# Attention probabilities in fp16 halves for all four key tiles: four in-place exponentials instead of two, and another order of scores on TensorE

## The chip, the cores and the metric

The kernel runs on one core of a Trainium2 chip. The metric is the device time of one execution in microseconds (us). TensorE (PE) multiplies, VectorE (DVE), ScalarE (ACT) and GpSimd (POOL) work on its results, SyncE (SP) issues the transfers. Matmuls write to PSUM, which has eight banks of 128 x 512 float32; everything else lies in SBUF.

## What is computed

Two transformer layers over x (2 batches x 512 rows x 512), each with modulated layer norms, attention and a feed-forward part. The change lies in the attention of layer 1:

```python
q_c = (c_q @ Wq_up).reshape(b, s, 128, 4);  q_r = (x @ Wq_rope).reshape(b, s, 128, 64)
k_c = (c_kv @ Wk_up).reshape(b, s, 128, 4); v_c = (c_kv @ Wv_up).reshape(b, s, 128, 4)
k_r = x @ Wk_rope
scores = (einsum('bqhd,bkhd->bhqk', q_c, k_c) + einsum('bqhd,bkd->bhqk', q_r, k_r)) / sqrt(68)
attn = softmax(scores);  out = einsum('bhqk,bkhd->bqhd', attn, v_c);  out @ Wo
```

There are 128 heads of 4 columns, with no mask: each query of 512 sees all 512 keys of its batch.

## The kernel before

The attention of layer 1 is cut into 128 units. A unit u is one pair of heads in one batch (u % 2). Per unit the scores are made turned, keys on the partitions: four key tiles of 128 keys times two heads give eight "slots" of 128 keys x 512 queries, in the order of the table `SLOTS` (slots 0 to 3 are key tiles 0 and 1, slots 4 and 5 key tile 2, slots 6 and 7 key tile 3). Work is handed on by hand-written semaphores; the order on each engine is that of the code. Nothing is scheduled by a tool.

**TensorE.** Per unit `before_sums` and then `behind_sums` run. Each slot's score is two matmuls into bank s % 4, with float32 operands in their rounded form: `scores1_rope` (L2593) and `scores1_content` (L2600). Between them stand three other kinds of work. `max_scores` (L2578) makes for unit u + 2 eight more score tiles with queries on the partitions, into banks 4 and 5 in turn, from which the row maxima are taken; number i of them waits until the maximum of number i - 2 is taken (`max_done`). `rope_queries` (L2508 to L2510) makes the queries of unit u + 3 in four pieces of three matmuls. `sum_unit` (L2623, L2628) multiplies the exponentials of unit u - 1 with its values into bank 7. It stands at the end of `before_sums`, that is behind slot 3's scores and number 1 of the maxima, and waits for POOL's semaphore `p_split` and DVE's `p_low`.

**The halves.** In the first 96 units (`HALVED`), the exponentials of key tiles 0 to 2 are split into two fp16 parts, high and rest, and multiplied with values that carry three bfloat16 parts in their columns: 12 matmuls of 128x32 by 128x512 (L2623). Key tile 3 is multiplied in float32, by 4 matmuls of 256 columns (L2628, two records each in the trace). Outputs go to four groups of 32 rows of bank 7.

**ScalarE** takes the exponential of each slot (L1413). Slots 0 to 3, 6 and 7 go to SBUF (x or pT, in turn by unit). Slots 4 and 5 (`IN_PLACE`) go back into their bank, and ScalarE copies them at once to fp16 (L1420). The high parts of slots 2 and 3 are ScalarE's too (L1424), behind slot 3. Ahead of a unit's exponentials it copies the rope queries of unit u + 2 (L1373, L1374, `q_high`).

**VectorE** takes the maxima of the eight tiles of unit u + 2 (L1934, called reduction i below), and makes the rest of slots 4 and 5 of unit u from the bank (L1925, `unit_low`), one behind reduction 4 and one behind reduction 5. Then comes one transposition (L1946) and the rest of the next rope queries (L1886, L1887, `q_low`). In every second unit there is a cast of weights (L1807) behind reduction 1. `unit_low` waits for the exponential of the slot behind its own, since only then has ScalarE's copy been made.

**GpSimd** makes both parts of slots 0 and 1 (L923, L925), prepares the values of the next unit, and makes the rests of slots 2 and 3 (L934), the last work for a unit's `sum_unit`.

Of the kernel before, what the change touches and what calls it, by code (L numbers as in the profile page):

```python
# [9 lines left out]
F16 = mybir.dt.float16  # L10
# [38 lines left out]
HTILES = 3  # L49
IN_PLACE = (4, 5)  # L50
# [21 lines left out]
def adaln_two_layers(nc, a, out):  # L72
# [8 lines left out]
    with ctx:  # L81
# [175 lines left out]
        halved_part = lambda par, s, i: pH[:, par, s, i] if s < 4 else pH_late[:, par, s - 4, i]  # L257
# [462 lines left out]
        def _(pool):  # L720
# [131 lines left out]
            def zero_others():  # L852

                pool.wait_ge(f_added, NT)
                pool.memset(ost[0:1, 0], 1.0).then_inc(zeroed, 1)
                pool.memset(vp[:], 0.0).then_inc(zeroed, 1)
                pool.memset(mcol[:].bitcast(F32), 0.0).then_inc(zeroed, 1)
                pool.wait_ge(zeroed, 3)
                for kp in range(2):
                    ones = slice(OROWS * kp + DEN, OROWS * kp + DEN + HD1)  # L860
                    pool.memset(vp[:, kp, HTILES:TB, :, ones], 1.0).then_inc(zeroed, 1)
                    pool.memset(vpb[:, kp, 0:HTILES, :, ones], 1.0).then_inc(zeroed, 1)

# [33 lines left out]
            def values(v, k, pair):  # L897
# [8 lines left out]
                pool.tensor_copy(vp[:, kp, HTILES:TB, :, OROWS * kp:OROWS * kp + HD1], full[:, HTILES:TB])  # L906
# [10 lines left out]
            def halve(u, k, pair):  # L917

                par = k % 2
                for i in range(2):  # L920
# [3 lines left out]
                    pool.wait_ge(p_split, 4 * u + i + 1)  # L924
# [7 lines left out]
                pool.wait_ge(exp1, 8 * u + 9)  # L932
                for i in range(2, 4):
                    e = pool.tensor_tensor(halved_part(par, i, 1), PT[par][:, i], halved_part(par, i, 0), ALU.subtract)  # L934
                e.then_inc(p_split, 1)
# [6 lines left out]
            pool.wait_ge(zeroed, 7)  # L942
# [148 lines left out]
        def _(act):  # L1091
# [284 lines left out]
            def period(u, k, pair):  # L1376
# [11 lines left out]
                for s in range(8):  # L1388
# [32 lines left out]
                    if s == 3 and exists(u, HALVED):  # L1421
                        act.wait_ge(exp1, 8 * u + 8)
                        for i in (2, 3):
                            act.activation(halved_part(k % 2, i, 0), PT[k % 2][:, i], ACT.Copy)  # L1424
# [86 lines left out]
        def _(dve):  # L1511
# [367 lines left out]
            dve.wait_ge(zeroed, 7)  # L1879
# [47 lines left out]
            def maxima(w, k, use, pair, p, quad):  # L1927


                if exists(w, UNITS):  # L1930
                    wait(dve, m_loaded[k % 2], 32 * use)
                    for i in range(8):
# [5 lines left out]
                        if i in IN_PLACE and exists(w - 2, HALVED):  # L1938
                            unit_low(w - 2, k - 2, i)
# [210 lines left out]
        def _(pe):  # L2150
# [429 lines left out]
            def scores1_rope(u, k, s, use):  # L2580

                if exists(u, UNITS):
# [7 lines left out]
                    if s + 4 in IN_PLACE and exists(u - 1, HALVED):  # L2590
                        pe.wait_ge(p_low, 2 * u - 1 + s)
# [10 lines left out]
            def sum_unit(w, k, pair):  # L2602

                if exists(w, UNITS):
# [12 lines left out]
                    if halved:  # L2617
                        pe.wait_ge(p_split, 4 * w + 4)
                        pe.wait_ge(p_low, 2 * w + 2)
                        for kb in range(HTILES):  # L2620
                            for h in range(2):
                                for half in range(2):
                                    pe.matmul(rows(2 * h + half), vpb[:, k % 2, kb, h], halved_part(k % 2, SLOTS.index((h, kb)), half),  # L2623
                                              start=(kb == 0 and opens), stop=False)
                        for h in range(2):
                            for half in range(2):
                                at = slice(half * S // 2, (half + 1) * S // 2)
                                e = pe.matmul(rows(2 * h + half)[:, at], vp[:, k % 2, HTILES, h], PT[k % 2][:, SLOTS.index((h, HTILES)), at],  # L2628
                                              start=False, stop=closes)
# [29 lines left out]
            def behind_sums(*turn):  # L2659
# [8 lines left out]
                queries(*turn, 1)  # L2668
                maximum(*turn, 4)
                scores(*turn, (6,))  # L2670
                queries(*turn, 2)
                maximum(*turn, 5)
                scores(*turn, (7,))
# [252 lines left out]
```

## Time and profile before

| | |
|---|---|
| three runs | 2174.14, 2176.51, 2177.23 us; median 2176.51 us |
| the profiled execution | 2175.61 us, of which 2173.8 us from the first to the last instruction |
| busy: PE, DVE, ACT, POOL | 98%, 80%, 62%, 62% of the span |
| mean granted clock of TensorE | 0.994 of full speed |

How to read the rows below: each names a line of the kernel, an engine, an operation, what it writes and reads, and how often it stands there in a row (xN). In a timeline the first number is the start, the second the time until the end of the last of the xN. What stands in brackets is the idle time just before, and what ended it. PEld is TensorE's load of weights, which runs beside its matmuls. TensorE's ends are modelled, and its starts are to be trusted more.

### The profile page before, as it was taken

The page shows a single profiled execution, that of the slowest core. Times are in us where ns is not written, and L with a number is a line of the kernel's source. Part 1 is how long each engine was busy: PE and PEld are TensorE (multiplying, and loading weights), DVE is VectorE, ACT ScalarE, POOL GpSimd, SP SyncE. Part 2 cuts the span into 40 slices and gives each one's busy share as a digit, 9 for nine tenths or more (in the row PEclk, how much of TensorE's full clock was granted, in tenths as well). Part 3 has the DMA queues.
Part 4 walks back from the last instruction along what each step waited for, and adds up shares of the span by engine and source line. Part 5 has one row for each costly group of instructions (what it writes and reads, how often), then busy time and mean ns, then how long its engine had stood idle before and what let it go on. Part 6 is the DMA issues. An engine that isn't in the chain of part 4 may idle for free.

```text
span 2173.8 us, 42824 instructions
## 1 busy us (share of the span) xinstructions
PE 2122.4 (98%) x11276; PEld 1644.1 (76%) x11276; DVE 1732.3 (80%) x3095; ACT 1341.9 (62%) x2709; POOL 1357.7 (62%) x1621
## 2 busy tenths in 40 slices
PE   7999999999999999999999999999999999999978
PEld 4788888888886757777777777777777777777756
DVE  6787788788777758888888888888888877788764
ACT  2443443433433568888888888888888865555532
POOL 4766766766753447777777777777777721365334
PEclk9999999999999999999999999999999999999999
DMA  7010010010004153222222222222222222444441
GB/s 249 26 43 30 20 48 29 19 48 29 19 20 121 37 189 108 71 73 78 74 78 65 77 78 74 76 66 79 75 77 69 75 79 76 138 130 124 114 130 40
DMA packets 138991, 165.82 MB, mean 76 GB/s; under 512 B 30261, under 2 KB 72917, under 8 KB 138916
## 3 DMA queue, kind: packets, MB, share of 16 engines
q1 hardware_dynamic: 135076, 152.31, 24.5%
q0 software_dynamic: 3840, 12.59, 2.0%
q8 instruction: 37, 0.61, 0.1%
q14 instruction: 38, 0.31, 0.0%
HBM read 101.52 MB, written 29.10 MB: 60 GB/s over the span
## 4 chain that ended last, share of the span: by engine, by line
PE 87%; DVE 7%; issue 2%; ACT 1%; POOL 1%; SPq 1%; DMA 1%; DVEq 0%; ACTq 0%; POOLq 0%
PE bank L2593 12%; PE bank L2578 11%; PE bank L2600 11%; PE bank L2155 7%; PE bank L2157 7%; PE bank L2156 7%; PE bank L2510 6%; PE bank L2508 5%; PE bank L2509 5%; PE bank L2623 3%; PE bank L2633 3%; PE bank L2628 2%; DVE rope_b L1631 1%; DVE rope_a L1630 1%; DVE rope_b L1632 1%
## 5 line engine op out<-in xcount | busy, mean ns | idle before, releaser
L1934 DVE TENSOR_REDUCE mcol<-bank 128x1 fp32r<-128x512 f32 x1024 | 684.1, 687 | 186.8 <-PE bank L2578 176.7
L2593 PE MATMUL bank<-q,k 128*128 128x512 f32 x1024 | 417.9, 408 | 0.0
L2578 PE MATMUL bank<-km,q 128*128 128x512 f32 x1024 | 406.0, 397 | 3.5 <-ACT q L1374 2.5
L2600 PE MATMUL bank<-q,k 128*128 128x512 f32 x1024 | 404.0, 395 | 0.0
L2578 PEld LDWEIGHTS bank<-km,q 128*128 128x128 f32 x1024 | 317.6, 310 | 53.0 <-DVE mcol L1934 3.9
L1413 ACT ACTIVATE pT<-bank 128x512 f32<-128x512 f32 x416 | 228.1, 602 | 113.7 <-PE bank L2600 111.9
L1413 ACT ACTIVATE x<-bank 128x512 f32<-128x512 f32 x416 | 227.7, 601 | 88.7 <-PE bank L2600 86.5
L2593 PEld LDWEIGHTS bank<-q,k 128*128 128x128 f32 x1024 | 192.3, 188 | 84.7 <-issue 27.9
L2600 PEld LDWEIGHTS bank<-q,k 128*128 128x128 f32 x1024 | 192.9, 188 | 31.7
L2510 PE MATMUL bank<-hT_hi,wr_lo 128*128 128x512 f32 x512 | 205.5, 401 | 0.0
L2508 PE MATMUL bank<-hT_hi,wr_hi 128*128 128x512 f32 x512 | 202.3, 395 | 0.1
L2509 PE MATMUL bank<-hT_lo,wr_hi 128*128 128x512 f32 x512 | 202.1, 395 | 0.0
L850 POOL TENSOR_TENSOR wr_lo<-wst,wr_hi 128x512 fp32r<-128x512 f32 x64 | 82.5, 1289 | 131.1 <-DVE wr_hi L1807 131.1
L2155 PE MATMUL bank<-hT_hi,w_hi 128*128 128x512 f32 x376 | 150.3, 400 | 0.0
L2157 PE MATMUL bank<-hT_hi,w_lo 128*128 128x512 f32 x376 | 148.5, 395 | 0.0
L2156 PE MATMUL bank<-hT_lo,w_hi 128*128 128x512 f32 x376 | 148.4, 395 | 0.0
L744 POOL TENSOR_TENSOR bq_lo<-rope_a,bq_hi 128x512 fp32r<-128x512 f32 x64 | 83.3, 1302 | 82.0 <-ACT bq_hi L1145 82.0
L923 POOL CAST pH<-x 128x512 f16<-128x512 f32 x96 | 58.8, 612 | 118.6 <-ACT x L1413 118.6
L736 POOL TENSOR_TENSOR rope_a<-rope_a,rope_b 128x512 f32<-128x512 f32 x80 | 105.8, 1323 | 43.2 <-DVE rope_b L1632 43.2
L1925 DVE TENSOR_TENSOR pH_late<-bank,pH_late 128x512 f16<-128x512 f32 x192 | 131.3, 684 | 1.5
L1413 ACT ACTIVATE bank<-bank 128x512 f32<-128x512 f32 x192 | 112.0, 583 | 19.7 <-PE bank L2600 19.7
L925 POOL TENSOR_TENSOR pH<-x,pH 128x512 f16<-128x512 f32 x96 | 117.8, 1227 | 7.7
(372 smaller groups left out, 5061.5 us busy)
## 6 DMA issues: line engine op xcount, KB each, us to landing
q<-q SPq DMA_DIRECT2D x256, 128.0 KB, 2.3
wst<-in_L_attn_Wq_rope SPq DMA_DIRECT2D x64, 256.0 KB, 3.1
o_d<-ost SPq DMA_DIRECT2D x63, 256.0 KB, 3.1
st_q<-in_L_attn_wq SPq DMA_DIRECT2D x8, 1024.0 KB, 7.6
st_wo<-in_L_attn_wo SPq DMA_DIRECT2D x8, 1024.0 KB, 5.4
q<-qc_d SPq DMA_DIRECT2D x256, 32.0 KB
km<-kc_d SPq DMA_DIRECT2D x256, 32.0 KB
k<-kc_d SPq DMA_DIRECT2D x256, 32.0 KB
```

What stands on the lines that cost most here:

```text
L1413: act.activation(bank[s % 4][:] if in_place else PT[k % 2][:, s], bank[s % 4][:], ACT.Exp, scale=float((HD1 + ROPE) ** -0.5)).then_inc(exp ...
L1925: dve.tensor_tensor(halved_part(k % 2, s, 1), bank[s % 4][:], halved_part(k % 2, s, 0), ALU.subtract).then_inc(p_low, 1)
L1934: dve.tensor_reduce(mcol[:, k % 2, i % 4, i // 4:i // 4 + 1], bank[4 + i % 2][:], AX.X, ALU.max, negate=True)\
L2155: pe.matmul(ps, lh_, rh, start=(i == 0), stop=False)
L2156: pe.matmul(ps, lh_, rl, start=False, stop=False)
L2157: e = pe.matmul(ps, ll, rh, start=False, stop=(i == n - 1))
L2508: pe.matmul(bank[6][:], wr_hi[:, par, kk], hT_hi[:, kk, at], start=(kk == 0), stop=False)
L2509: pe.matmul(bank[6][:], wr_hi[:, par, kk], hT_lo[:, kk, at], start=False, stop=False)
L2510: e = pe.matmul(bank[6][:], wr_lo[:, par, kk], hT_hi[:, kk, at], start=False, stop=(kk == KT - 1))
L2578: pe.matmul(bank[4 + i % 2][:], q2[:, k % 4, h, i % 4:S:4], km[:, b, h], start=True, stop=True).then_inc(max_mm, 1)
L2593: pe.matmul(bank[s % 4][:], k1[:, k % 2, t], q1[:, k % 4, h], start=True, stop=False)
L2600: pe.matmul(bank[s % 4][:], k2[:, k % 2, h, t], q2[:, k % 4, h], start=False, stop=True).then_inc(scores1, 1)
```

## The change

`HTILES` becomes 4: key tile 3 is multiplied in fp16 halves too, so the 4 float32 matmuls of 256 columns become 4 fp16 ones of 512 columns. `IN_PLACE` becomes slots 2 to 5. Their exponentials stay in their banks; ScalarE makes the high part and VectorE the rest, so VectorE has four of these a unit instead of two. They stand where the new table `LOW_BEHIND` puts them: behind reductions 0, 2, 4 and 5. Slots 6 and 7 go to SBUF as before and are split there: ScalarE casts slot 6 between the exponentials of slots 6 and 7, GpSimd casts slot 7 and makes both rests, once slot 7's exponential is there. The score of slot 6 now waits for the rest of slot 2 (`p_low`), which shares its bank, and that of slot 7 for the rest of slot 3. On TensorE the scores of slots 6 and 7 move ahead of the maxima tiles 4 and 5.

```diff
-HTILES = 3
-IN_PLACE = (4, 5)
+HTILES = 4
+IN_PLACE = (2, 3, 4, 5)
+LOW_BEHIND = {0: 2, 2: 3, 4: 4, 5: 5}
...
-        halved_part = lambda par, s, i: pH[:, par, s, i] if s < 4 else pH_late[:, par, s - 4, i]
+        halved_part = lambda par, s, i: (
+            pH[:, par, s, i] if s < 4 else pH_late[:, par, s - 4, i] if s < 6
+            else PT[par][:, s - 2].bitcast(F16)[:, i * S:(i + 1) * S])
...
-                pool.tensor_copy(vp[:, kp, HTILES:TB, :, OROWS * kp:OROWS * kp + HD1], full[:, HTILES:TB])
...
-                pool.wait_ge(exp1, 8 * u + 9)
-                for i in range(2, 4):
-                    e = pool.tensor_tensor(halved_part(par, i, 1), PT[par][:, i], halved_part(par, i, 0), ALU.subtract)
-                e.then_inc(p_split, 1)
+                pool.wait_ge(exp1, 8 * u + 12)
+                pool.sem_inc(spare, 1)
+                pool.tensor_copy(halved_part(par, 7, 0), PT[par][:, 7]).then_inc(p_split, 1)
+                pool.tensor_tensor(halved_part(par, 6, 1), PT[par][:, 6], halved_part(par, 6, 0), ALU.subtract)
+                pool.wait_ge(p_split, 5 * u + 4)
+                pool.tensor_tensor(halved_part(par, 7, 1), PT[par][:, 7], halved_part(par, 7, 0), ALU.subtract).then_inc(p_split, 1)
...
-                    if s == 3 and exists(u, HALVED):
-                        act.wait_ge(exp1, 8 * u + 8)
-                        for i in (2, 3):
-                            act.activation(halved_part(k % 2, i, 0), PT[k % 2][:, i], ACT.Copy)
+                    if s == 6 and exists(u, HALVED):
+                        act.wait_ge(exp1, 8 * u + 11)
+                        act.activation(halved_part(k % 2, 6, 0), PT[k % 2][:, 6], ACT.Copy)
...
-                        if i in IN_PLACE and exists(w - 2, HALVED):
-                            unit_low(w - 2, k - 2, i)
+                        if i in LOW_BEHIND and exists(w - 2, HALVED):
+                            unit_low(w - 2, k - 2, LOW_BEHIND[i])
...
-                        pe.wait_ge(p_low, 2 * u - 1 + s)
+                        pe.wait_ge(p_low, 4 * u - 1 + s)
+                    if s - 4 in IN_PLACE and exists(u, HALVED):
+                        pe.wait_ge(p_low, 4 * u - 5 + s)
...
-                        for h in range(2):
-                            for half in range(2):
-                                at = slice(half * S // 2, (half + 1) * S // 2)
-                                e = pe.matmul(rows(2 * h + half)[:, at], vp[:, k % 2, HTILES, h], PT[k % 2][:, SLOTS.index((h, HTILES)), at],
-                                              start=False, stop=closes)
...
-                maximum(*turn, 4)
                 scores(*turn, (6,))
+                maximum(*turn, 4)
                 queries(*turn, 2)
-                maximum(*turn, 5)
                 scores(*turn, (7,))
+                maximum(*turn, 5)
                 maximum(*turn, 6)
```

VectorE, one unit with its cast of weights, behind the loop. In the names `mcol` holds the maxima, `pH` and `pH_late` the fp16 parts, `q` the queries. Before:

```order
L1886 TENSOR_TENSOR q<-bank,q 64x512
L1887 TENSOR_TENSOR q<-bank,q 64x512
L1934 TENSOR_REDUCE mcol<-bank 128x1 x2
L1807 CAST wr_hi<-wst 128x512
L1934 TENSOR_REDUCE mcol<-bank 128x1 x3
L1925 TENSOR_TENSOR pH_late<-bank,pH_late 128x512
L1934 TENSOR_REDUCE mcol<-bank 128x1
L1925 TENSOR_TENSOR pH_late<-bank,pH_late 128x512
L1934 TENSOR_REDUCE mcol<-bank 128x1 x2
L1946 STREAM_TRANSPOSE mrow<-mcol 128x4x32
```

The same unit on VectorE, now:

```order
L1889 TENSOR_TENSOR q<-bank,q 64x512
L1936 TENSOR_REDUCE mcol<-bank 128x1
L1927 TENSOR_TENSOR pH<-bank,pH 128x512
L1936 TENSOR_REDUCE mcol<-bank 128x1
L1809 CAST wr_hi<-wst 128x512
L1936 TENSOR_REDUCE mcol<-bank 128x1
L1927 TENSOR_TENSOR pH<-bank,pH 128x512
L1936 TENSOR_REDUCE mcol<-bank 128x1 x2
L1927 TENSOR_TENSOR pH_late<-bank,pH_late 128x512
L1936 TENSOR_REDUCE mcol<-bank 128x1
L1927 TENSOR_TENSOR pH_late<-bank,pH_late 128x512
L1936 TENSOR_REDUCE mcol<-bank 128x1 x2
```

A rest (slot 2's) now stands between reductions 0 and 1, and another (slot 3's) behind reduction 2.

TensorE, the second half of a unit, from maximum tile 3 (L2578) to the last piece of the queries. Before:

```order
L2578 MATMUL bank<-km,q 128x512
L2593 MATMUL bank<-q,k 128x512
L2600 MATMUL bank<-q,k 128x512
L2508 MATMUL bank<-hT_hi,wr_hi 128x512
L2509 MATMUL bank<-hT_lo,wr_hi 128x512
L2510 MATMUL bank<-hT_hi,wr_lo 128x512
L2578 MATMUL bank<-km,q 128x512
L2593 MATMUL bank<-q,k 128x512
L2600 MATMUL bank<-q,k 128x512
L2508 MATMUL bank<-hT_hi,wr_hi 128x512
L2509 MATMUL bank<-hT_lo,wr_hi 128x512
L2510 MATMUL bank<-hT_hi,wr_lo 128x512
```

The same place on TensorE now, from maximum tile 3 (L2580) on:

```order
L2580 MATMUL bank<-km,q 128x512
L2597 MATMUL bank<-q,k 128x512
L2604 MATMUL bank<-q,k 128x512
L2510 MATMUL bank<-hT_hi,wr_hi 128x512
L2511 MATMUL bank<-hT_lo,wr_hi 128x512
L2512 MATMUL bank<-hT_hi,wr_lo 128x512
L2597 MATMUL bank<-q,k 128x512
L2604 MATMUL bank<-q,k 128x512
L2580 MATMUL bank<-km,q 128x512
L2510 MATMUL bank<-hT_hi,wr_hi 128x512
L2511 MATMUL bank<-hT_lo,wr_hi 128x512
L2512 MATMUL bank<-hT_hi,wr_lo 128x512
```

Maximum tile 4 stood six matmuls behind tile 3 and now stands eight behind it, after the scores of slot 6.

GpSimd, the end of one unit's work. Before and now, with the two preparations of values (`l_pad`, `vp`) ahead of it:

```order
L912 CAST vp<-l_pad 128x6x4
L915 TENSOR_TENSOR vp<-l_pad,vp 128x6x4
L934 TENSOR_TENSOR pH<-x,pH 128x512 x2
```

```order
L913 CAST vp<-l_pad 128x8x4
L916 TENSOR_TENSOR vp<-l_pad,vp 128x8x4
L935 CAST x<-x 128x512
L936 TENSOR_TENSOR x<-x 128x512
L938 TENSOR_TENSOR x<-x 128x512
```

The cast of slot 7 has come in ahead of the two rests, and all three now start behind the exponential of slot 7 instead of that of slot 4.

## Rows read from the trace of the kernel before

**Rows 1.** The page, part 1: busy time, share of the span, instructions by engine.

```profile
PE 2122.4 (98%) x11276; PEld 1644.1 (76%) x11276; DVE 1732.3 (80%) x3095; ACT 1341.9 (62%) x2709; POOL 1357.7 (62%) x1621
```

**Rows 2.** Timeline of TensorE around the first and the last halved sum.

```profile
828.25 0.62 PE L2623 MATMUL bank<-pH,vp 128*32 128x512 f16 x8
...
1756.85 0.62 PE L2623 MATMUL bank<-pH,vp 128*32 128x512 f16 x8
```

**Rows 3.** Timeline of TensorE, one sum in the middle of the loop.

```profile
1111.38 0.40 PE L2578 MATMUL bank<-km,q 128*128 128x512 f32 x1
1111.70 0.62 PE L2623 MATMUL bank<-pH,vp 128*32 128x512 f16 x8
1112.15 0.39 PE L2623 MATMUL bank<-pH_late,vp 128*32 128x512 f16 x4
1112.36 0.60 PE L2628 MATMUL bank<-pT,vp 128*32 128x256 f32 x8
1112.90 0.50 PE L2593 MATMUL bank<-q,k 128*128 128x512 f32 x1
1113.24 0.40 PE L2600 MATMUL bank<-q,k 128*128 128x512 f32 x1
```

**Rows 4.** Timeline of VectorE, from reduction 4 to reductions 0 and 1 of the next.

```profile
1106.45 0.69 DVE L1934 TENSOR_REDUCE mcol<-bank 128x1 fp32r<-128x512 f32 x1 [0.70 <-PE bank L2578]
1107.17 0.69 DVE L1925 TENSOR_TENSOR pH_late<-bank,pH_late 128x512 f16<-128x512 f32 x1
1107.84 0.69 DVE L1934 TENSOR_REDUCE mcol<-bank 128x1 fp32r<-128x512 f32 x1
1108.45 0.68 DVE L1925 TENSOR_TENSOR pH_late<-bank,pH_late 128x512 f16<-128x512 f32 x1
1109.05 1.28 DVE L1934 TENSOR_REDUCE mcol<-bank 128x1 fp32r<-128x512 f32 x2
1110.36 0.40 DVE L1946 STREAM_TRANSPOSE mrow<-mcol 128x128 f32<-128x128 f32 x1
1110.86 0.68 DVE L1886 TENSOR_TENSOR q<-bank,q 64x512 fp32r<-64x512 f32 x1
1111.55 0.69 DVE L1887 TENSOR_TENSOR q<-bank,q 64x512 fp32r<-64x512 f32 x1
1112.28 1.29 DVE L1934 TENSOR_REDUCE mcol<-bank 128x1 fp32r<-128x512 f32 x2
```

**Rows 5.** Timeline ahead of the loop, where a maximum tile waits for a reduction.

```profile
790.29 1.28 DVE L1934 TENSOR_REDUCE mcol<-bank 128x1 fp32r<-128x512 f32 x2
...
791.03 0.31 PEld L2578 LDWEIGHTS bank<-km,q 128*128 128x128 f32 x1 [0.94 <-DVE mcol L1934]
...
791.48 0.39 PE L2508 MATMUL bank<-hT_hi,wr_hi 128*128 128x512 f32 x1
```

**Rows 6.** Timeline of ScalarE, from the rope queries to slot 5.

```profile
1109.25 0.59 ACT L1373 ACTIVATE q<-bank 64x512 fp32r<-64x512 f32 x1 [0.34 <-PE bank L2510]
...
1110.47 2.07 ACT L1413 ACTIVATE x<-bank 128x512 f32<-128x512 f32 x4
...
1113.63 0.58 ACT L1408 ACTIVATE ost<-bank 128x512 f32<-128x512 f32 x1
1114.11 0.59 ACT L1413 ACTIVATE bank<-bank 128x512 f32<-128x512 f32 x1
1114.73 0.60 ACT L1420 ACTIVATE pH_late<-bank 128x512 f16<-128x512 f32 x1
1115.29 0.58 ACT L1413 ACTIVATE bank<-bank 128x512 f32<-128x512 f32 x1
```

**Rows 7.** Timeline of GpSimd in the same unit.

```profile
1111.24 0.61 POOL L923 CAST pH<-x 128x512 f16<-128x512 f32 x1 [2.50 <-ACT x L1413]
1111.93 1.16 POOL L925 TENSOR_TENSOR pH<-x,pH 128x512 f16<-128x512 f32 x1
...
1117.62 2.30 POOL L934 TENSOR_TENSOR pH<-x,pH 128x512 f16<-128x512 f32 x2
```

More of the change, by code:

```diff
@@ L860, in zero_others @@
                     ones = slice(OROWS * kp + DEN, OROWS * kp + DEN + HD1)
-                    pool.memset(vp[:, kp, HTILES:TB, :, ones], 1.0).then_inc(zeroed, 1)
                     pool.memset(vpb[:, kp, 0:HTILES, :, ones], 1.0).then_inc(zeroed, 1)
@@ L923, in halve @@
                     pool.tensor_copy(halved_part(par, i, 0), PT[par][:, i]).then_inc(p_split, 1)
-                    pool.wait_ge(p_split, 4 * u + i + 1)
+                    pool.wait_ge(p_split, 5 * u + i + 1)
                     e = pool.tensor_tensor(halved_part(par, i, 1), PT[par][:, i], halved_part(par, i, 0), ALU.subtract)
@@ L941, in _ @@
             pool.wait_ge(vc_ready, NT)
-            pool.wait_ge(zeroed, 7)
+            pool.wait_ge(zeroed, 5)
             values(0, 0, 0)
@@ L1878, in _ @@
             key_low(1)
-            dve.wait_ge(zeroed, 7)
+            dve.wait_ge(zeroed, 5)
             dve.wait_ge(vc_ready, NT)
@@ L2617, in sum_unit @@
                     if halved:
-                        pe.wait_ge(p_split, 4 * w + 4)
-                        pe.wait_ge(p_low, 2 * w + 2)
+                        pe.wait_ge(p_split, 5 * w + 5)
+                        pe.wait_ge(p_low, 4 * w + 4)
                         for kb in range(HTILES):
@@ L2622, in sum_unit @@
                                 for half in range(2):
-                                    pe.matmul(rows(2 * h + half), vpb[:, k % 2, kb, h], halved_part(k % 2, SLOTS.index((h, kb)), half),
-                                              start=(kb == 0 and opens), stop=False)
-                        for h in range(2):
-                            for half in range(2):
-                                at = slice(half * S // 2, (half + 1) * S // 2)
-                                e = pe.matmul(rows(2 * h + half)[:, at], vp[:, k % 2, HTILES, h], PT[k % 2][:, SLOTS.index((h, HTILES)), at],
-                                              start=False, stop=closes)
+                                    e = pe.matmul(rows(2 * h + half), vpb[:, k % 2, kb, h], halved_part(k % 2, SLOTS.index((h, kb)), half),
+                                                  start=(kb == 0 and opens), stop=(kb == HTILES - 1 and closes))
                     else:
@@ L2668, in behind_sums @@
                 queries(*turn, 1)
+                scores(*turn, (6,))
                 maximum(*turn, 4)
-                scores(*turn, (6,))
                 queries(*turn, 2)
+                scores(*turn, (7,))
                 maximum(*turn, 5)
-                scores(*turn, (7,))
                 maximum(*turn, 6)
```

## The prediction, made before the changed kernel had run

> **What bounds the kernel now.** I read the page first: PE is busy 98% of the span, DVE 80%, ACT and POOL 62% [rows 1]. That is a mean over the whole program, so I looked for the stage that the change touches. The first halved sum starts at 828.25 us and the 96th at 1756.85 [rows 2]: 95 units in 928.6 us, 9.775 us each. In the timeline of TensorE inside it, matmul follows matmul. From maximum tile 1 (1111.38) over the sum to the second matmul of slot 4 (1113.24) it is 1.86 us [rows 3]. The other 34 of the 36 full matmuls of a unit then have 9.775 - 1.86 = 7.915 us, 0.2328 us each, with no wait among them. So TensorE alone sets the pace, and what others do is hidden. How well hidden shows on VectorE: it waits 0.70 us for maximum tile 4 [rows 4], but reductions 0 and 1 start at 1112.28, 0.58 us behind the start of the sum, although their tiles were made before it (the second's matmul started at 1111.38 [rows 3]). So VectorE is already late there, and catches up by waiting at tiles 2 to 4. That is where the change puts work.
>
> **TensorE's own work.** The 12 fp16 matmuls run from 1111.70 to 1112.36: three rounds of four column groups, 0.22 us each. The 4 float32 matmuls take from 1112.36 to about 1112.79, and the next full matmul starts at 1112.90, 0.54 behind 1112.36 [rows 3]. The float32 part alone has no row of its own end. I take the way out of the column groups (0.11) as unchanged, so 0.43 goes and one fp16 round of 0.22 comes: 0.21 less. TensorE's floor is 9.565 us. With nothing else changed that would be 95 x 0.21 = 20 us of gain.
>
> **VectorE's work.** Two more rests a unit. A rest is 0.68 to 0.69 us long, but the next operation starts before its end: 1108.45 to 1109.05 is 0.60, and the pair of reductions (1.28 for two of 0.69) gives 0.60 too. Behind reduction 4 I see 0.72 [rows 4]. I take 0.60 to 0.61, since most follow at that, and keep 0.72 for the range. The other steps: from the pair at 1109.05 to the transposition 1.31, so 0.71 from reduction 7; then 0.50, 0.69 and 0.73 to the first reduction [rows 4]. Twelve operations, a transposition and two query rests are 12 x 0.605 + 0.11 + 0.50 + 0.69 + 0.73 = 9.3 us, under 9.565: VectorE has room on average. The question is where its work stands.
>
> **The order, laid out with these rows.** Put 0 at the start of a sum. The second matmul of slot 4 starts at 1.33 (1.54 before, less 0.21). Maximum tile 3 is five matmuls on, 2.49. Tile 4 is now eight behind it, 4.36; tile 5 six behind that, 5.75; tile 7 at 6.92; the next sum at 9.565. A reduction starts 0.43 behind its matmul's start (0.39 and a handoff of 0.04). So reduction 4 starts at 4.79, slot 4's rest at 5.40, reduction 5 with its tile at 6.18, slot 5's rest at 6.79, reductions 6 and 7 at 7.39 and 7.99, transposition 8.70, query rests 9.20 and 9.89, reduction 0 at 10.62. That is 1.05 behind the next sum; it was 0.58. Then slot 2's rest at 1.65 and reduction 1 only at 2.25. Tile 3 shares its bank with tile 1, so it waits for reduction 1's end at 2.94 plus 0.05. TensorE would be there at 2.49: **it waits 0.50 us**. A wait costs more than itself. Where a maximum tile waited for a reduction, its weights were loaded only then (791.03), and the next matmul started 0.45 behind, instead of 0.23 [rows 5]: 0.22 more. Behind tile 3 stand the scores of slots 5 to 7, the other tiles and the queries, all later by 0.72. Since tile 4 is eight behind tile 3, VectorE doesn't catch up: its reduction 4 waits for this tile, and the loop closes. Checked round: reduction 1 0.69 + handoff 0.05 + 0.45 + 7 x 0.2328 + 0.43 = 3.25 to reduction 4; from there to the next reduction 1 7.03 (the list above). The sum is 10.28 a unit. The cast of every second unit falls where VectorE waits for tile 4 (from reduction 1 it is ready at 2.41, with the cast at 2.9, needed at 3.25), so I cost it at nothing; without that cover it is 0.46.
>
> A page of the Trainium skill speaks of the reload: TensorE: Matmul & The Clock Gate, section LDWEIGHTS, has a load depend on the number of columns alone, some 107 ns for 128. By it the loop would be an estimated 10.17 us. The trace disagrees: the maximum tile's load is 0.31 us.
>
> **ScalarE.** It gets one cast more, but the order matters: slot 2's rest waits for the exponential of slot 3, and ahead of that stand now two exponentials and a copy in place of two exponentials. The last query matmul (6.69, end 7.09) releases the two query copies (0.61 each [rows 6]), exponential 0 starts at -1.22 against the next sum, each next 0.49 on (2.07 for four), in place to copy 0.62, copy to the next 0.56 [rows 6]: exponential 3 ends at 1.52. The handoff is 0.05 to 0.18 (GpSimd started 0.18 behind an exponential's end [rows 6, 7]). So slot 2's rest could start at 1.57 to 1.70, and VectorE comes at 1.65: a second loop almost as long, 10.20 to 10.32 when closed through tile 3. I take VectorE's 10.28. The output copy of every second unit (0.48 [rows 6]) stands behind slot 3 and delays slots 4 and 5 only, which have room; nothing. The cast of slot 6 lies in the wait for slot 7's score; nothing as well.
>
> **GpSimd.** It loses the 0.2 us copy of values, and its last work is now a cast and two rests behind exponential 7. Cast to rest 0.69, rest to rest 1.13, the last 1.17 [rows 7], with 0.18 of handoff 3.17 us. Exponential 7 ends at 6.56 (slot 7's second matmul 5.52, +0.44, +0.60), so the sum could start at 9.73 instead of 9.565. In the stalled order both move by 0.72, so the sum is late by 0.17; that fits in the 0.50 in which TensorE would wait at tile 3, and costs nothing. Without that stall it is 0.17 to 0.29 a unit (in units with the output copy exponential 7 ends 0.12 later).
>
> **The sum.** (10.28 - 9.775) x 95 = 48 us slower. Against the profiled execution, 2175.6 + 48 = 2223.6; the median of the runs shown is 0.9 us above it. I say 2224 us. The float32 and fp16 parts are in it already, since the loop no longer passes TensorE's floor. Outside the 96 units nothing moves that I can price: two small memsets go.
>
> **The rivals.**
> 1. VectorE keeps up, and GpSimd sets the sum (the other side). If VectorE's chain from reduction 4 to reduction 1 were 6.53 us or less instead of 7.03, tile 3 would not wait. The point from which the result is no slower is a loop of 9.775. For it: no row shows the new order, and handoffs may be shorter. Against: it needs eleven steps of measured length to be 0.045 shorter each. The unit is then 9.73 to 9.85 by GpSimd's chain, so 2171 to 2183, and I call it no change. Chance 0.07.
> 2. All waits hidden, TensorE at its floor: 9.565, 2155.6 us. For it: the busiest engine does have less work. Against: both VectorE and GpSimd must be faster than their rows. Chance 0.08, with all that is faster.
> 3. Only part of the stall: the reload costs 0.11 as behind the sum, or is absorbed. Then 10.0 to 10.15, 2197 to 2211. This lies in the forecast's own range.
> 4. VectorE doesn't overlap its operations in the new order. Then each next one starts at the former's end. Five pitches on the loop grow from 0.60 to 0.69 (the two ahead of reduction 5 are covered by its wait), 10.28 + 0.45 = 10.73, 2266 us. For it: one rest did follow at 0.72. Against: five rows at 0.60 or near. Chance 0.08, with all that is above 2245.
>
> Rival 4 is what the Trainium skill states in VectorE: DVE Perf Modes, section The DRAIN you can't avoid: the next operation doesn't start until the pipe is empty. The rows of pairs in 1.28 us disagree.
>
> **How the numbers follow.** The forecast, with the stall at tile 3, has 0.77; its own range is 2197 (reload and one handoff less) to 2245 (two pitches of 0.72 a unit, 0.23 more: +22). With 0.77 there and the edges of the others, 2190 to 2245 holds some 0.8. A change of 0.2%, 4 us, is about what a measurement of this kernel can tell from none. Faster 0.08, within 0.2% 0.06, slower 0.86.
>
> **What would show it.** In the new trace the unit should be 10.2 to 10.3 us from sum to sum. TensorE's weight load of the maxima (L2580) should wait for `mcol`, once a unit at tile 3, 0.3 to 0.6 us, and perhaps at tile 2. Reduction 0 should start about 1 us behind the sum, slot 2's rest right behind it. The four matmuls of the new round should be 0.2 us apart from the ones before. GpSimd's last rest should end just about where the sum starts. The prediction is wrong if VectorE's rests are much shorter, if `mcol` isn't waited for, or if the wait stands at the sum itself (GpSimd) or at slots 6 and 7 (the rests of slots 2 and 3, which I have ready over 1 us early).

## The result, and the profile after

The changed kernel takes **2242.88 us** (median of 4 runs, 2240.74 to 2244.87); the kernel before took 2175.32 us. The ratio is 1.031, with a 95% interval of 1.030 to 1.032: 67.6 us slower.

The page after, part 1, as [rows 1]: PE still shows 98%, so the share says nothing of the loss. VectorE's busy time has grown by 120 us.

```profile
PE 2190.2 (98%) x10892; PEld 1631.5 (73%) x10892; DVE 1852.6 (83%) x3287; ACT 1405.1 (63%) x2805; POOL 1399.1 (62%) x1619
```

The timeline of TensorE around the first and the last halved sum, as [rows 2]:

```profile
828.83 0.62 PE L2627 MATMUL bank<-pH,vp 128*32 128x512 f16 x8
...
1815.04 0.62 PE L2627 MATMUL bank<-pH,vp 128*32 128x512 f16 x8
```

Between them lie 95 units in 986.21 us, 10.381 each instead of 9.775. That is 57.6 us of the span's growth of 69.3 (2243.1 against 2173.8). The other 11.7 lie outside: 0.6 before the first sum, 0.7 in the unit in which the halved part ends, 5.8 from the 97th to the 127th sum (312.3 against 306.5 us, 10.41 a unit against 10.22), and 4.6 from there to the end. The stretch from the 97th sum on has no halves at all; only the order of TensorE is new there. (Its means take in two shorter units at the end; a unit in its middle takes 10.65, where it was 10.45.) Most of the last 4.6 us is one wait for a transfer of weights, behind the last sum (TensorE, before and after):

```profile
2080.58 1.97 PE L2732 MATMUL bank<-ident,bw 128*128 128x128 f32 x16 [0.82 <-DMA bw<-in_L_ffn_base_W]
2148.49 2.71 PE L2731 MATMUL bank<-ident,bw 128*128 128x128 f32 x16 [3.98 <-DMA bw<-in_L_ffn_base_W]
```

The mean granted clock behind the 127th sum is also a little lower, 0.91 of full speed against 0.95; both are means of the levels 2.4 and 1.2 GHz. In the runs below this stretch takes between 99.2 and 104.2 us whatever was changed (105.3 here, 100.7 before), so I don't count it to the change.

The places of TensorE's waits in one unit after, as [rows 3] (timelines of PE and PEld, put together in order of time):

```profile
1105.77 0.31 PEld L2580 LDWEIGHTS bank<-km,q 128*128 128x128 f32 x1 [0.29 <-DVE mcol L1936]
1106.23 0.43 PE L2597 MATMUL bank<-q,k 128*128 128x512 f32 x1
...
1108.68 0.62 PE L2627 MATMUL bank<-pH,vp 128*32 128x512 f16 x8
1109.12 0.39 PE L2627 MATMUL bank<-pH_late,vp 128*32 128x512 f16 x4
1109.34 0.39 PE L2627 MATMUL bank<-pT,vp 128*32 128x512 f16 x4
1109.66 0.50 PE L2597 MATMUL bank<-q,k 128*128 128x512 f32 x1
...
1110.23 0.55 PE L2580 MATMUL bank<-km,q 128*128 128x512 f32 x1
1110.61 0.39 PE L2510 MATMUL bank<-hT_hi,wr_hi 128*128 128x512 f32 x1
...
1111.08 0.40 PE L2512 MATMUL bank<-hT_hi,wr_lo 128*128 128x512 f32 x1
1111.47 0.31 PEld L2580 LDWEIGHTS bank<-km,q 128*128 128x128 f32 x1 [0.44 <-DVE mcol L1936]
1111.93 0.39 PE L2597 MATMUL bank<-q,k 128*128 128x512 f32 x1
```

The sum is shorter as laid out: 0.98 from its start to the next full matmul, where it was 1.20. Three places lose more than that. Each is counted as the distance from one start to the next beyond the usual 0.2328. Tile 3 (1111.47): 0.16 of wait and 0.23 of late load. Tile 2 (1110.23): 0.15. Tile 7 (1105.77): 0.23, and 0.04 at the matmul behind. That is 0.81, and 9.565 + 0.81 = 10.375; measured are 10.35 from tile 3 to tile 3 here and 10.381 on the mean.

VectorE in the same stretch (its timeline), from reduction 4 to the cast, as [rows 4]:

```profile
1103.63 0.69 DVE L1936 TENSOR_REDUCE mcol<-bank 128x1 fp32r<-128x512 f32 x1 [0.77 <-PE bank L2580]
1104.23 0.68 DVE L1927 TENSOR_TENSOR pH_late<-bank,pH_late 128x512 f16<-128x512 f32 x1
1105.02 0.69 DVE L1936 TENSOR_REDUCE mcol<-bank 128x1 fp32r<-128x512 f32 x1
1105.63 0.68 DVE L1927 TENSOR_TENSOR pH_late<-bank,pH_late 128x512 f16<-128x512 f32 x1
1106.23 1.28 DVE L1936 TENSOR_REDUCE mcol<-bank 128x1 fp32r<-128x512 f32 x2
1107.54 0.42 DVE L1948 STREAM_TRANSPOSE mrow<-mcol 128x128 f32<-128x128 f32 x1
1107.99 0.68 DVE L1888 TENSOR_TENSOR q<-bank,q 64x512 fp32r<-64x512 f32 x1
1108.68 0.69 DVE L1889 TENSOR_TENSOR q<-bank,q 64x512 fp32r<-64x512 f32 x1
1109.41 0.69 DVE L1936 TENSOR_REDUCE mcol<-bank 128x1 fp32r<-128x512 f32 x1
1110.13 0.69 DVE L1927 TENSOR_TENSOR pH<-bank,pH 128x512 f16<-128x512 f32 x1
1110.74 0.68 DVE L1936 TENSOR_REDUCE mcol<-bank 128x1 fp32r<-128x512 f32 x1
1111.34 0.96 DVE L1809 CAST wr_hi<-wst 128x512 fp32r<-128x512 f32 x1
```

Reduction 1 ends at 1111.42, and tile 3's weights load at 1111.47. Slot 2's rest (1110.13) follows reduction 0 by 0.72, slots 4's and 5's follow theirs by 0.60 and 0.61. The units around it are alike at this place: tile 3's loads stand at 1101.12, 1111.47, 1121.82 and 1132.23. From sum to sum it is less even, 10.2 to 10.6 us in turns of four units, but where one sum is late, the wait at tile 2 behind it is shorter. The pace is set at tile 3, by VectorE.

GpSimd's last three operations before the sum, as [rows 7] (its timeline):

```profile
1105.55 0.61 POOL L935 CAST pT<-pT 128x512 f16<-128x512 f32 x1 [2.48 <-ACT pT L1416]
1106.12 1.17 POOL L936 TENSOR_TENSOR pT<-pT 128x512 f16<-128x512 f32 x1
1107.25 1.18 POOL L938 TENSOR_TENSOR pT<-pT 128x512 f16<-128x512 f32 x1
```

They end at 1108.43, 0.25 ahead of the sum at 1108.68, which is where TensorE comes anyway (0.33 behind tile 1's matmul at 1108.35, as before: 0.32 [rows 3]). So GpSimd is close to being waited for, and isn't in this unit.

Reduction 0 starts 0.73 behind the sum (1109.41), not 1.05 as forecast, because tile 7 has already held the sum back.

### The profile page after: what moved, and what is told of

It reads as the page before. It is cut to its first block, busy times and chain, and to the rows that moved or that the text cites. A ratio compares the mean times of both kernels' runs of the same rounds, so it can differ in the third digit from the quotient of the medians.

```text
span 2243.1 us, 43218 instructions
## 1 busy us (share of the span) xinstructions
PE 2190.2 (98%) x10892; PEld 1631.5 (73%) x10892; DVE 1852.6 (83%) x3287; ACT 1405.1 (63%) x2805; POOL 1399.1 (62%) x1619
## 4 chain that ended last, share of the span: by engine, by line
PE 87%; DVE 7%; issue 2%; ACT 1%; DMA 1%; POOL 1%; SPq 0%; DVEq 0%; ACTq 0%; POOLq 0%
PE bank L2580 14%; PE bank L2597 12%; PE bank L2604 10%; PE bank L2157 7%; PE bank L2159 7%; PE bank L2158 6%; PE bank L2512 5%; PE bank L2511 5%; PE bank L2510 5%; PE bank L2627 4%; PE bank L2632 2%; DVE rope_b L1633 1%; DVE rope_a L1632 1%; DVE rope_b L1634 1%; PE bank L2293 1%
## 5 line engine op out<-in xcount | busy, mean ns | idle before, releaser
L2580 PE MATMUL bank<-km,q 128*128 128x512 f32 x1024 | 450.9, 461 | 4.7 <-ACT q L1377 2.4
L2597 PE MATMUL bank<-q,k 128*128 128x512 f32 x1024 | 419.2, 409 | 0.0
L2580 PEld LDWEIGHTS bank<-km,q 128*128 128x128 f32 x1024 | 307.4, 309 | 129.5 <-DVE mcol L1936 99.7
L2597 PEld LDWEIGHTS bank<-q,k 128*128 128x128 f32 x1024 | 194.5, 190 | 105.5 <-issue 71.8
L1416 ACT ACTIVATE bank<-bank 128x512 f32<-128x512 f32 x384 | 228.2, 594 | 68.7 <-PE bank L2604 67.5
L1416 ACT ACTIVATE pT<-bank 128x512 f32<-128x512 f32 x320 | 180.6, 599 | 72.5 <-PE bank L2604 64.1
L1416 ACT ACTIVATE x<-bank 128x512 f32<-128x512 f32 x320 | 181.0, 599 | 45.9 <-PE bank L2604 37.2
L1927 DVE TENSOR_TENSOR pH<-bank,pH 128x512 f16<-128x512 f32 x192 | 131.4, 684 | 4.8 <-ACT bank L1416 1.9
L1423 ACT ACTIVATE pH_late<-bank 128x512 f16<-128x512 f32 x192 | 114.7, 597 | 6.1
```

Source lines behind the costliest of these rows:

```text
L1416: act.activation(bank[s % 4][:] if in_place else PT[k % 2][:, s], bank[s % 4][:], ACT.Exp, scale=float((HD1 + ROPE) ** -0.5)).then_inc(exp ...
L1927: dve.tensor_tensor(halved_part(k % 2, s, 1), bank[s % 4][:], halved_part(k % 2, s, 0), ALU.subtract).then_inc(p_low, 1)
L2580: pe.matmul(bank[4 + i % 2][:], q2[:, k % 4, h, i % 4:S:4], km[:, b, h], start=True, stop=True).then_inc(max_mm, 1)
L2597: pe.matmul(bank[s % 4][:], k1[:, k % 2, t], q1[:, k % 4, h], start=True, stop=False)
```

## The experiments

All times are medians, with the ratio to the kernel before run on the same chip and its 95% interval. A unit's time is the mean between the first and the 96th halved sum of the profiled execution; "behind" is that from the 97th to the 127th. The ratios of e1 to e4 are to one set of runs of the kernel before, those of e5, e7 and e8 to another, those of e9 and e10 to a third. What stands below about units rests on one profiled execution each.

| run | us | ratio | a halved unit | behind |
|---|---|---|---|---|
| before | 2175.3 to 2177.2 | 1 | 9.775 | 10.22 |
| changed | 2242.9 | 1.031 (1.030 to 1.032) | 10.381 | 10.41 |
| e1_old_order | 2246.0 | 1.032 (1.030 to 1.033) | 10.469 | 10.22 |
| e2_rests_later | 2206.0 | 1.014 (1.012 to 1.017) | 9.994 | 10.41 |
| e3_query_swap | 2233.3 | 1.026 (1.025 to 1.028) | 10.267 | 10.41 |
| e4_before_new_order | 2211.0 | 1.016 (1.015 to 1.018) | 10.061 | 10.41 |
| e5_all_three | 2197.7 | 1.010 (1.008 to 1.012) | 9.994 | 10.17 |
| e7_tile7_later | 2237.1 | 1.028 (1.026 to 1.030) | 10.389 | 10.17 |
| e8_before_tile7_later | 2197.5 | 1.010 (1.007 to 1.012) | 9.985 | 10.17 |
| e9_other_layout | 2174.3 | 0.998 (0.997 to 0.999) | 9.727 | 10.21 |
| e10_slot7_later | 2191.2 | 1.006 (1.004 to 1.008) | 9.928 | 10.20 |

**e1_old_order: the changed kernel with TensorE's old order.**

```diff
-                scores(*turn, (6,))
                 maximum(*turn, 4)
+                scores(*turn, (6,))
                 queries(*turn, 2)
-                scores(*turn, (7,))
                 maximum(*turn, 5)
+                scores(*turn, (7,))
```

> The changed kernel (2242.9 us; 10.38 us a halved unit, 10.26 from sum to sum behind unit 96) with TensorE's old order of the scores of slots 6 and 7 and maximum tiles 4 and 5, everything else as changed. Theory A: the new order puts tile 7 five matmuls (1.16 us) behind tile 5, just as long as the reduction of tile 5 needs (0.43 + 0.69 + 0.05), so its weights are loaded late, 0.2 us a unit in every unit; and it puts tile 4 two matmuls later, on the loop that goes through VectorE. With the old order the units behind 96 should go back to about 10.07, and the halved ones to 10.1 to 10.25 (VectorE's work in units with the cast, or GpSimd's in front of the sum, is next): 2215 to 2225 us. Theory B: the two rests more on VectorE cost all of it and the order nothing: about 2243 us. Theory C: the order was needed so that exponential 7 comes early: the sum waits for GpSimd 0.2 to 0.5 us more, 2245 to 2260 us.

Half of A came: the units behind 96 are back at 10.22, that of the kernel before (not at 10.07). But the halved ones got slower, 10.47, and the whole, 2246.0, is no faster than the changed kernel; that is theory C's time. The waits of the weight loads over one unit and a little more:

```profile
1108.59 0.31 PEld L2580 LDWEIGHTS bank<-km,q 128*128 128x128 f32 x1 [0.46 <-DVE mcol L1936]
1116.19 0.12 PEld L2627 LDWEIGHTS bank<-pH,vp 128*32 128x32 bf16 x8 [0.51 <-POOL pT L938]
1118.84 0.31 PEld L2580 LDWEIGHTS bank<-km,q 128*128 128x128 f32 x1 [0.45 <-DVE mcol L1936]
```

Tile 7 is no longer there. Tile 3 still waits, and now the sum waits for GpSimd (0.51 idle, where 0.25 is usual), as theory C says. That wait isn't what sets the unit, since tile 3 behind it still waits for VectorE. VectorE itself waits for ScalarE (their timelines, put together):

```profile
1106.51 0.59 ACT L1416 ACTIVATE bank<-bank 128x512 f32<-128x512 f32 x1
1107.25 0.69 DVE L1927 TENSOR_TENSOR pH<-bank,pH 128x512 f16<-128x512 f32 x1 [0.21 <-ACT bank L1416]
...
1116.77 0.59 ACT L1416 ACTIVATE bank<-bank 128x512 f32<-128x512 f32 x1
1117.50 0.69 DVE L1927 TENSOR_TENSOR pH<-bank,pH 128x512 f16<-128x512 f32 x1 [0.40 <-ACT bank L1416]
1118.11 0.68 DVE L1936 TENSOR_REDUCE mcol<-bank 128x1 fp32r<-128x512 f32 x1
1118.71 1.30 DVE L1809 CAST wr_hi<-wst 128x512 fp32r<-128x512 f32 x1
```

In every halved unit slot 2's rest starts 0.14 to 0.15 behind the end of slot 3's exponential. This is the prediction's second loop, and it closes: 0.61 to reduction 1, 0.68 + 0.05 to tile 3, 4.41 to the last query matmul, 0.44 to ScalarE's copy of the queries, 3.33 to exponential 3, 0.59 + 0.14 to the next rest, together 10.25. The units without a cast take just that, 10.24 to 10.28. Those with a cast take about 10.67: the cast (1118.71) lasts 1.30, reduction 2 behind it is late, and tile 4's load waits as well, 0.42 in all. In the changed kernel tile 4 comes two matmuls later and its load doesn't wait. So in the halved units the new order more than pays for itself, by 0.09 a unit, though not through GpSimd.

**e2_rests_later: slot 2's and 3's rests behind reductions 2 and 3.**

```diff
-LOW_BEHIND = {0: 2, 2: 3, 4: 4, 5: 5}
+LOW_BEHIND = {2: 2, 3: 3, 4: 4, 5: 5}
```

> The changed kernel with the rests of slots 2 and 3 behind reductions 2 and 3 instead of 0 and 2. Theory A (the stall at maximum tile 3 is what slot 2's rest between reductions 0 and 1 costs): TensorE no longer waits 0.4 us at tile 3 and loads its weights in time; what is left is tile 7's late load, GpSimd in front of the sum and perhaps slot 6's score waiting for slot 2's rest: 9.85 to 10.05 us a halved unit, 2190 to 2210 us. Theory B (VectorE has simply too much work, wherever it stands): the wait moves to slot 6's or slot 7's score at the same size, 10.3 to 10.4 a unit, 2235 to 2245 us.

Theory A: 0.39 us a unit comes back, 37 us in all, with the same number of operations on VectorE. The wait at tile 3 is gone; its load starts one matmul ahead again:

```profile
1112.28 0.31 PEld L2580 LDWEIGHTS bank<-km,q 128*128 128x128 f32 x1
```

Both rests were moved, but tile 3 waits for reduction 1, and only slot 2's rest stood in front of that. So it was the place of this rest, between reductions 0 and 1, that cost 0.39 of the 0.61.

**e3_query_swap: the query rest on the upper partitions first.**

```diff
-                    dve.tensor_tensor(q1[ROPE:P, k % 4, 0], bank[6][0:ROPE], q2[0:ROPE, k % 4, 0].bitcast(F32), ALU.subtract)
                     dve.tensor_tensor(q1[0:ROPE, k % 4, 1], bank[6][ROPE:P], q2[ROPE:P, k % 4, 1].bitcast(F32), ALU.subtract)\
+                    dve.tensor_tensor(q1[ROPE:P, k % 4, 0], bank[6][0:ROPE], q2[0:ROPE, k % 4, 0].bitcast(F32), ALU.subtract)\
                        .then_inc(q1_split, 1)
```

> The changed kernel with the two rests of the rope queries on VectorE in the other order, so that the last one before reduction 0 reads the lower partitions. Slot 2's rest follows reduction 0 at 0.72 us in the changed kernel, others at 0.60. Theory A: it is held until reduction 0 has ended because the last operation that read SBUF (the query rest on the upper 64 partitions) started in another group of partitions. Then the swap gives 0.60, 0.12 us less on the loop: 10.25 a halved unit, about 2231 us. Theory B: the 0.72 is a wait for ScalarE's exponential of slot 3: it stays, and the time too, 2243 us.

Theory A: 10.381 to 10.267, 0.114 less, where 0.12 was forecast. The timelines of VectorE and ScalarE:

```profile
1109.46 0.59 ACT L1416 ACTIVATE bank<-bank 128x512 f32<-128x512 f32 x1
1109.59 0.69 DVE L1936 TENSOR_REDUCE mcol<-bank 128x1 fp32r<-128x512 f32 x1
1110.20 0.69 DVE L1927 TENSOR_TENSOR pH<-bank,pH 128x512 f16<-128x512 f32 x1
```

The rest now follows by 0.61. The 0.72 was not a wait for ScalarE but VectorE holding an operation until the one before it had ended. The Trainium skill has this rule, in VectorE: DVE Perf Modes, section "Two Vector instructions with no wait between them": an operation is held, among other cases, if its first SBUF input starts in another group of 32 partitions than that of the last operation that read SBUF. Reduction 0 reads PSUM alone, so the query rest on the upper 64 partitions was still the last one. The trace agrees, with this swap. It also agrees with the 0.72 behind reduction 4 in [rows 4]: that unit has no cast, which reads SBUF from partition 0 on. In the kernel before, slot 4's rest follows reduction 4 by 0.61 in all 47 halved units with a cast and by 0.72 in 47 of 48 without one.

The swap gave all that it could. Exponential 3 ends at 1110.05 and the rest starts 0.15 behind it, where 0.14 is what e1 shows of a rest that waits for it: the loop through ScalarE now closes at the same length as VectorE's.

**e4_before_new_order: the kernel before with the new order alone** (the diff of e1 the other way round).

> The kernel before with only TensorE's new order of scores and maximum tiles. Theory A: tile 7 waits for the reduction of tile 5 and its weights load late, 0.2 to 0.25 us in each unit, since TensorE is the bound there: halved units 9.98 to 10.02, the units behind about 10.26, together 22 + 6 us: 2200 to 2206 us. Theory B: the order costs nothing by itself: 2175 us.

Theory A in kind, with more in size: 35 us, 0.286 a halved unit, where 0.21 to 0.25 was forecast. Put into the kernel before, the order alone costs more than half of what the whole change does. Timeline of that kernel:

```profile
1105.48 0.63 PE L2578 MATMUL bank<-km,q 128*128 128x512 f32 x2
...
1105.91 0.69 DVE L1934 TENSOR_REDUCE mcol<-bank 128x1 fp32r<-128x512 f32 x1
...
1106.66 0.31 PEld L2578 LDWEIGHTS bank<-km,q 128*128 128x128 f32 x1 [0.29 <-DVE mcol L1934]
```

Tile 5's matmul starts at 1105.48, its reduction at 1105.91 and ends at 1106.60; tile 7's load at 1106.66. TensorE would have come to tile 7's matmul at 1106.64 (1105.48 + 5 x 0.2328), so there is no wait to speak of. But the weights of a matmul that isn't held load one matmul earlier, beside the one before (its load then starts 0.23 ahead). Here they start with the wait's end, and the next matmul comes 0.22 to 0.29 late.

**e7_tile7_later: the changed kernel, tile 7 behind the next unit's slot 0.**

```diff
-                scores(*turn, range(3))
+                scores(*turn, (0,))
+                max_scores(turn[0] + 1, turn[1] + 1, 7, turn[2](1))
+                scores(*turn, (1, 2))
...
-                maximum(*turn, 7)
```

> The changed kernel with maximum tile 7 alone moved behind the next unit's score of slot 0. Theory A: in the halved units TensorE's late load at tile 7 lies beside VectorE's longer chain, which sets the pace through tile 3; so its removal gives nothing there (10.33 to 10.40 a unit), and 0.19 us in each of the units behind 96: 2233 to 2239 us. Theory B: the late loads add up, 0.26 us a unit comes back: 10.12, 2210 to 2218 us.

Theory A, in both stretches: 10.389 instead of 10.381, and 10.17 instead of 10.41 behind. A stall of 0.27 us on the busiest engine was taken away in every halved unit, and nothing came back there. It lay beside VectorE's chain, and TensorE only waited longer at tile 2 (mostly 0.38 to 0.45 in the waits of its loads, where it was at most 0.28).

**e8_before_tile7_later: the same in the kernel before with the new order.**

> The kernel before with the new order of scores and maximum tiles, and tile 7 moved behind the next unit's score of slot 0. With the new order alone it took 2211 us, 10.06 a halved unit. Theory A: all of that is tile 7, which is five matmuls behind tile 5; seven behind, its weights load in time, and the unit is 9.775 again: 2173 to 2178 us. Theory B: another part of the order (tile 4 later, slots 6 and 7 earlier) costs some of it: 2185 us or more.

Theory B. Of the 0.286 only 0.076 comes back. The timeline shows what is next:

```profile
1105.94 0.69 DVE L1934 TENSOR_REDUCE mcol<-bank 128x1 fp32r<-128x512 f32 x1
1106.55 0.68 DVE L1925 TENSOR_TENSOR pH_late<-bank,pH_late 128x512 f16<-128x512 f32 x1
1107.15 1.28 DVE L1934 TENSOR_REDUCE mcol<-bank 128x1 fp32r<-128x512 f32 x2
...
1110.32 1.29 DVE L1934 TENSOR_REDUCE mcol<-bank 128x1 fp32r<-128x512 f32 x2
...
1111.07 0.31 PEld L2578 LDWEIGHTS bank<-km,q 128*128 128x128 f32 x1 [0.18 <-DVE mcol L1934]
```

Reduction 5 starts 1105.94. Behind it seven operations go without a gap to reduction 0, which ends at 1111.01, and tile 2 waits for that. Tile 2 to tile 5 on TensorE and tile 5 to its reduction close the loop. Its length is 4.38 (reduction 5 to reduction 0) + 0.69 + 0.15 to tile 2's matmul (1111.16) + 4.32 to tile 5's (1115.48) + 0.43 = 9.97, the unit. The new order puts two more matmuls between tiles 2 and 5, and this loop becomes longer than TensorE's own work, even with the two rests a unit of the kernel before.

**e5_all_three: e2, e3 and e7 together.**

> The changed kernel with three mends at once: the rests of slots 2 and 3 behind reductions 2 and 3, the query rests in the other order, and maximum tile 7 moved behind the next unit's score of slot 0 (seven matmuls behind tile 5 instead of five). Theory A: what is left of the stalls of the run with later rests (9.99 us a unit) is tile 7's late load (0.26) and GpSimd in front of the sum (up to 0.17); without the first the unit is 9.70 to 9.80, the units behind 96 are back at about 10.22: 2167 to 2180 us, no better than before though TensorE has 0.2 us less to do. Theory B: VectorE's work itself (9.7 to 9.8 us a unit with the cast) or GpSimd's is the bound beyond that: 9.85 to 9.95, 2182 to 2195 us. Theory C: with the stalls gone TensorE's floor of 9.565 shows: 2156 us.

None of the three in full; B's mechanism was nearest, but in which order VectorE's chain closes was still open. The unit is 9.994, exactly that of e2, although the hold and tile 7's late load are gone. It is the loop of e8 again: tile 2 waits 0.39 to 0.44 for reduction 0.

**e9_other_layout: tile 5, and slots 6 and 7, earlier.** On top of e5 (shown is TensorE's order behind the sum; the table puts the rests of slots 2 and 3 both behind reduction 2):

```diff
-                scores(*turn, (4,))
+                scores(*turn, (4, 5))
                 maximum(*turn, 2)
                 queries(*turn, 0)
                 maximum(*turn, 3)
-                scores(*turn, (5,))
                 queries(*turn, 1)
-                scores(*turn, (6,))
                 maximum(*turn, 4)
-                queries(*turn, 2)
-                scores(*turn, (7,))
+                scores(*turn, (6, 7))
                 maximum(*turn, 5)
+                queries(*turn, 2)
                 maximum(*turn, 6)
                 queries(*turn, 3)
```

> The changed kernel with tile 7 behind the next unit's slot 0 and the query rests swapped, as in the run with three mends, but laid out so that tiles 4 to 7 and slots 6 and 7 all come early: TensorE does slots 4 and 5 together, tiles 2 and 3, two query pieces, tile 4, slots 6 and 7 together, tile 5; VectorE makes the rests of slots 2 and 3 one behind the other after reduction 2. Theory A: the run with three mends was held at 9.99 us a unit by the chain from tile 5's reduction through seven more VectorE operations to reduction 0 and tile 2, because the new order puts tile 5 late; here tile 5 is 3 matmuls earlier and tile 2 two later, GpSimd gets exponential 7 0.7 us earlier, and the unit comes to VectorE's total of 9.6 to 9.75: 2160 to 2176 us. Theory B: VectorE's total with its cast beside GpSimd is the bound at 9.85 to 10.0 whatever the layout: 2183 to 2198 us.

Theory A. The unit is 9.727, under the 9.775 of the kernel before, and the time 2174.3 us (12 runs) against 2177.2: a ratio of 0.998, just clear of 1. The stretch from 1000 to 1200 us of three kernels (columns: us, then busy us and instructions of PE, PEld, DVE, ACT, POOL, clock, DMA share, GB/s), the kernel before first:

```profile
1000.00:1200.00 200.00, 200.00 (x1147) 156.36 (x1149) 173.11 (x278) 165.59 (x297) 151.05 (x235) 1.00 0.29 77
```

the changed kernel:

```profile
1000.00:1200.00 200.00, 199.98 (x1001) 144.23 (x1000) 187.96 (x300) 168.83 (x300) 150.32 (x221) 1.00 0.26 70
```

and this one:

```profile
1000.00:1200.00 200.00, 200.00 (x1065) 154.09 (x1064) 193.31 (x320) 175.73 (x319) 161.54 (x239) 1.00 0.28 77
```

VectorE is now busy 97% of the time; its one longer idle time, 0.31 us, comes in units without a cast. The weight loads still wait once a unit, at tile 5, and lose 0.19 there:

```profile
1108.66 0.31 PEld L2581 LDWEIGHTS bank<-km,q 128*128 128x128 f32 x1 [0.23 <-DVE mcol L1936]
```

That is about what keeps the unit above TensorE's 9.565. Whether a layout without this late load comes nearer to it, with VectorE so full, was not tried.

**e10_slot7_later: as e9, but slot 7's score behind tile 5 and a query piece,** and the rests of slots 2 and 3 behind reductions 2 and 3, as in e5:

```diff
-LOW_BEHIND = {2: (2, 3), 4: (4,), 5: (5,)}
+LOW_BEHIND = {2: 2, 3: 3, 4: 4, 5: 5}
...
-                scores(*turn, (6, 7))
+                scores(*turn, (6,))
                 maximum(*turn, 5)
                 queries(*turn, 2)
+                scores(*turn, (7,))
```

> As the run before it, but with the single rests behind reductions 2 and 3, and slot 7's score behind tile 5 and a query piece instead of straight behind slot 6's. Exponential 7 is then 0.9 us later, 0.23 later than in the changed kernel's order. Theory A: GpSimd's cast and two rests (3.3 us from exponential 7 to the sum) now set the sum: a wait there of 0.2 to 0.4 us, 9.9 to 10.0 a unit, 2187 to 2198 us. Theory B (VectorE's total is the bound in both): the same time as the run before it.

Theory A. The unit is 9.928, and the only load that waits longer than 0.1 us for another engine is the sum's, for GpSimd:

```profile
1101.63 0.12 PEld L2627 LDWEIGHTS bank<-pH,vp 128*32 128x32 bf16 x8 [0.54 <-POOL pT L938]
```

## Why the prediction was right, and where not

**TensorE's own work** was right within a hundredth: the sum is 0.22 us shorter in the trace, 0.21 forecast.

**The stall at tile 3** was right in place, releaser and mechanism. Forecast were a wait of 0.50 and a late load of 0.22; measured are 0.16 and 0.23, with 0.15 already lost at tile 2 and 0.27 at tile 7. I had put the whole of VectorE's lag at the last place where it can be waited for. e2 confirms that the place of slot 2's rest is the cause of 0.39 us a unit. Tile 7 was not foreseen at all.

**The length of the loop** was the term mis-sized: forecast 10.28, measured 10.381 (10.35 in the unit shown; the rest is not traced step by step). The rest behind reduction 0 follows by 0.72, not 0.60: +0.12, which e3 took away again. The step to the query rests was 0.45, not 0.50: -0.05. The reading of [rows 4] showed one such 0.72 and I put it to the range, as if it came by chance; e3 shows that it has a cause. The cast was costed at nothing, and in the changed kernel that holds within 0.05: VectorE comes to tile 4 just in time behind it, without idle time. In e1 it did not hold.

**ScalarE's exponential of slot 3** as a second loop of 10.20 to 10.32 was right: it measures 10.25 (e1). It doesn't bound the changed kernel. In the unit shown exponential 3 ends at 1109.87 and the rest starts at 1110.13, 0.26 behind, where 0.14 would do; and e3 moved that rest nearer to its reduction, which a wait for ScalarE would have forbidden. It bounds e1, and e3 comes up to it.

**GpSimd** was right: 2.88 us for its three operations and 0.16 of handoff, 3.04 against 3.17 forecast, just in time in the changed kernel, and the bound in e10, where exponential 7 comes later and no other load waits for long.

**"Outside the 96 units nothing moves that I can price"** was wrong. TensorE's new order holds in all units, and costs 0.19 us a unit behind the 96th, 5.8 us (e7 gets it back). The step that failed is the check of tile 7. My own list had reduction 5 at 6.18, so ending at 6.87, and tile 7 at 6.92: just in time by starts. I did not ask whether a matmul that is released just in time still has its weights loaded in time. It hasn't: up to 0.23 us are lost when the release comes less than one matmul ahead.

**The sum**: 57.6 us in the 96 units (48 forecast), 5.8 behind them and 0.7 between (0), and 5.2 us at the start and in the end stage, which vary from run to run. The time, 2242.9, stayed in the range by 2 us, and that is partly luck. The upper end of 2245 was worked out from two operations held a unit, 22 us. One was held, 11 us; the rest of the room was used up by tile 7 and by the ends of the program, which the range had not been made for.

**The rivals.** VectorE keeping up (rival 1) and TensorE at its floor (rival 2) did not come, and e9 shows what rival 1 needs: another order on both engines. A cheaper reload (rival 3) did not come either: it cost 0.23 at tiles 3 and 7. That VectorE doesn't overlap at all (rival 4) is wrong; of the rests it fails to overlap one, for the reason that e3 shows. Here the prediction read the Trainium skill by half: the section that it names in VectorE: DVE Perf Modes, The DRAIN you can't avoid, adds that a next operation that is not held starts earlier, so the rows of pairs in 1.28 us don't speak against it. What stays open is how much of the 0.81 us at tiles 3, 2 and 7 belongs to the rests and how much to the order. They are not a sum: the order alone costs 0.29, taking it back costs 0.09, and moving the rests gives 0.39.

## What to carry to other kernels

When engines hand tiles to each other in a fixed order, write down where each tile is released and taken, and follow every loop round once: an operation that is put in front of a release costs its length even where its engine has idle time later. Taking a stall away on the busiest engine gives nothing while another engine's chain closes at the same length (e7), so look for the longest loop, not the longest wait, and know the next one: ScalarE's loop, 0.10 us shorter, took over in e1. And a release that comes just in time is late for the load of the weights: keep one matmul of distance.

## What the runs showed of the hardware

- A matmul that was released late started its weight load with the release, and the next one followed by 0.45 to 0.46 us instead of 0.23. Behind the sum, with contiguous weights (L2597), the next one followed by 0.34 [rows 3]. The load of the maxima, whose columns lie four elements apart, takes 0.31 us, the other loads of 128 columns 0.19.
- VectorE's next operation follows by 0.60 us when it isn't held, by 0.69 to 0.73 when it is, for operations of 0.68 to 0.69 us. In e3 it was the operation two back, the last to read SBUF, that decided it.
- The weight cast on VectorE, SBUF to SBUF, has a median of 427 ns in the kernel before and 925 in the changed one. In the unit shown it starts at 1111.34, while a rest of GpSimd runs from 1110.86 to 1112.02, and it ends at 1112.30, 0.28 behind that. In the halved units of the changed kernel all 47 casts end 0.28 behind such a rest. The Trainium skill states in SBUF — State Buffer, section Who interferes with whom, that a cast of VectorE can need the pair of ports that it shares with GpSimd, and that whoever issues first keeps it; the trace agrees. In the changed kernel this costs at most 0.05 in a unit with a cast, because it takes up the time in which VectorE would wait for tile 4. In e1 the cast takes 1.29 to 1.32 us, and reduction 2 behind it is late for tile 4.
